# A routed mixture of experts with a gated recurrence on one core: seventeen early pairs instead of eighteen, a setup without transfers between partitions, and two statistics moved

## The reference

```python
combined = xn @ W_in + b_in                      # 256 + 8 columns
embed, state_in = combined[..., :256], combined[..., 256:]
gate = sigmoid(combined @ W_g + b_g)             # 8 columns
state[t] = gate[t] * state[t-1] + (1 - gate[t]) * state_in[t]
s = concat(embed, states) @ W_out + b_out
# mixture of experts: 32 experts, 4 per token, from the best 4 of 8 groups
w, idx = gate_top_k(softmax(xn @ wg.T))          # weights sum to one
# an expert takes at most 1280 rows, in the order of the tokens
y = sum over experts of w * (silu(xe @ w1) * (xe @ w3)) @ w2
z = (silu(xn @ sw1) * (xn @ sw3)) @ sw2          # shared expert
out = x + s * silu(y + z)
```

## Time and profile before

| | |
|---|---|
| three runs | 1102.82, 1106.45, 1108.12 us (median 1106.45) |
| the profiled execution | 1105.46 us, its span 1103.5 us |
| PE busy | 1003.9 us (91%) |
| DVE, ACT, POOL busy | 775.6 (70%), 550.2 (50%), 721.3 us (65%) |
| mean granted TensorE clock | 0.959 of full speed |
| DMA | 197.5 MB, 179 GB/s over the span |

### The profile page before, as it was taken

The page is one execution under the profiler, slowest core; times in us unless marked ns, Lnnn a source line. Parts: engine busy times, 40 slices in busy tenths (PEclk is TensorE's granted clock), DMA queues, the critical chain, the costliest instruction groups (busy, mean ns, idle before and its releaser), DMA issues.

```text
span 1103.5 us, 29611 instructions
## 1 busy us (share of the span) xinstructions
PE 1003.9 (91%) x8031; PEld 957.7 (87%) x8031; DVE 775.6 (70%) x2472; ACT 550.2 (50%) x1039; POOL 721.3 (65%) x564
## 2 busy tenths in 40 slices
PE   7899999999860899899999999999999999999784
PEld 5888888988760899899999999999999999999741
DVE  5888888887760577677777766776777777777574
ACT  4776778777530344344444434444444444445343
POOL 2077777777777766765787876666666667666340
PEclk8899999999995799999999999999999999999987
DMA  9634444444343898787888988898788988877969
GB/s 261 208 127 143 142 143 143 141 149 143 133 145 126 267 234 171 145 196 156 179 168 185 212 157 169 181 202 175 156 186 201 204 203 188 181 145 153 248 152 345
DMA packets 177521, 197.50 MB, mean 179 GB/s; under 512 B 20449, under 2 KB 169234, under 8 KB 177426
## 3 DMA queue, kind: packets, MB, share of 16 engines
q1 hardware_dynamic: 123344, 124.92, 38.0%
q0 software_dynamic: 53440, 71.50, 34.3%
q10 hardware_dynamic: 642, 0.02, 0.0%
HBM read 96.88 MB, written 103.13 MB: 181 GB/s over the span
## 4 chain that ended last, share of the span: by engine, by line
PE 62%; POOL 16%; issue 7%; DVE 6%; DMA 3%; ACT 2%; SPq 1%; DVEq 0%; POOLq 0%; ACTq 0%
POOL slot_rows L854 16%; PE h L989 12%; PE h L991 12%; PE h L990 12%; PE yb L1007 6%; PE yb L1009 6%; PE yb L1008 6%; PE xt L973 6%; DMA raw<-L_ffn_w 1%; DVE s_all L1976 1%; DMA y_sum<-y_more,y_idx 1%; ACT acth L1319 1%; DVE raw L1601 0%; PE h L1198 0%; PE h L1202 0%
## 5 line engine op out<-in xcount | busy, mean ns | idle before, releaser
L989 PE MATMUL h<-xh,w_hl 128*128 (+1 forms) x1392 | 411.8, 296 | 7.2 <-DVE xl L1578 5.6
L991 PE MATMUL h<-xl,w_hl 128*128 (+1 forms) x1392 | 394.7, 284 | 0.0
L990 PE MATMUL h<-xh,w_hl 128*128 (+1 forms) x1392 | 393.6, 283 | 0.0
L1319 ACT ACTIVATE acth<-act 128x512 fp32r<-128x512 f32 x174 | 109.9, 632 | 334.1 <-PE yb L1009 294.2
L989 PEld LDWEIGHTS h<-xh,w_hl 128*128 128x128 f32 x1392 | 265.2, 191 | 9.3 <-issue 8.8
L990 PEld LDWEIGHTS h<-xh,w_hl 128*128 128x128 f32 x1392 | 265.4, 191 | 0.0
L991 PEld LDWEIGHTS h<-xl,w_hl 128*128 128x128 f32 x1392 | 265.1, 190 | 0.0
L1588 DVE TENSOR_TENSOR actl<-act,acth 128x512 fp32r<-128x512 f32 x174 | 120.6, 693 | 178.4 <-ACT acth L1319 178.1
L1007 PE MATMUL yb<-w_hl,acth 128*128 128x256 f32 x696 | 200.3, 288 | 13.3 <-DVE y_more L1848 7.4
L834 POOL DMA_INDIRECT y_sum<-x_all,y_idx x98 | 156.1, 1593 | 73.5 <-DVE x_all L1848 48.6
L1009 PE MATMUL yb<-w_hl,actl 128*128 128x256 f32 x696 | 198.4, 285 | 0.0
(11 more groups left out here) (238 smaller groups left out, 1591.4 us busy)
## 6 DMA issues: line engine op xcount, KB each, us to landing
rows<-slot_rows SPq DMA_DIRECT2D x121, 289.0 KB, 3.9
raw<-L_ffn_w SPq DMA_DIRECT2D x105, 256.0 KB, 4.1
slot_rows<-rows SPq DMA_DIRECT2D x32, 289.0 KB
x_all<-L_attn_x SPq DMA_DIRECT2D x16, 512.0 KB, 6.3
x_all<-L_attn_x SPq DMA_DIRECT2D x32, 256.0 KB
out<-s_all SPq DMA_DIRECT2D x32, 256.0 KB, 4.0
y_sum<-yw SPq DMA_DIRECT2D x31, 256.0 KB
x_all<-slot_rows SPq DMA_DIRECT2D x21, 289.0 KB, 4.2
```

The costliest lines, as they stand in the source:

```text
L989: mm(out, high, xh[:, k, cols], start=(k == 0), stop=False)
L990: mm(out, low, xh[:, k, cols], start=False, stop=False)
L991: ins = mm(out, high, xl[:, k, cols], start=False, stop=(k == KD - 1))
L1319: av(acth[:, :], act[:, :], ACT.Copy).then_inc(acth_ready, 2)
```

## The change

- Expert 0 has two early pairs instead of three; its third pair is done in the late stage, ahead of its last. The y buffers of early and late pairs move accordingly, and so do the waits for them.
- The zero stores of the early experts are issued one expert at a time between the loads, in place of four together and then two.
- POOL waits for a group's four indices at once, in place of one tile at a time.
- The low part of the bias goes into row 64 of `wo`, which DVE can write itself, and the rows 0 to 15 are made in one DVE instruction from two loaded copies of the eight rows: high part times +1 or -1, plus the copy times 0 or 1, by columns that POOL's iota gives. Both transfers and their wait go.
- The statistics of groups 2 and 3 stand in the setup on DVE, and the first half of group 1's normalisation behind the second pair's `xhigh` on ACT.
- `SOON` is 16 in place of 20.

```diff
-SOON = 20
+SOON = 16
-EARLY_PAIRS = 3 * FIRST
+EARLY_COUNTS = (2, 3, 3, 3, 3, 3)
+EARLY_LIST = [(e, j) for e in range(FIRST) for j in range(EARLY_COUNTS[e])]
+EARLY_PAIRS = len(EARLY_LIST)
...
-        LATE_FIFTH, LATE_LAST = (SET_A + 3, SET_A + 4), (SET_A + 1, SET_A + 2)
+        LATE_THIRD = SET_A + 1
+        LATE_FOURTH = (SET_A, SET_A, SET_A + 2, SET_A + 3)
+        LATE_LAST = (SET_A + 2, SET_A + 3, SET_A + 4, SET_A + 1)
...
+        def early_splits(e, j):
+            return (2,) if j == 2 else (j,) if j < EARLY_COUNTS[e] - 1 else (1, 2)
+        def early_adds(e):
+            return 32 * (EARLY_COUNTS[e] - (e == 0))
...
-            sp.dma_start(s_wout8, w_out[D:D + SD, :]).then_inc(setup_loaded, 16)
+            for n in range(2):
+                sp.dma_start(s_wout16[n * SD:n * SD + SD, :], w_out[D:D + SD, :]).then_inc(setup_loaded, 16)
...
-            for e in range(PREFILLED, FIRST):
-                store_zeros(e)
-            load_early(5)
+            store_zeros(2)
+            load_early(5, sp.snap(zeros))
             load_raw(2, 1)
-            load_early(6, sp.snap(zeros))
             load_raw(2, 2)
+            load_early(6)
+            store_zeros(3)
+            load_raw(3, 0)
             load_early(7)
...
             for g in range(GROUPS):
                 slot = g % SLOTS
+                hold(dispatch_ready, GT * g + GT)
                 for t in range(GT):
-                    hold(dispatch_ready, GT * g + t + 1)
...
-                    if p == 0:
-                        pe.wait_ge(bias_moved, 32)
...
-            done(av(wo[0:SD, :], s_wout8, ACT.Copy))
+            done(av(high16.bitcast(F32R), s_wout16, ACT.Copy))
...
-            sc.dma_start(wo[97:98, :].bitcast(F32), bias_low).then_inc(bias_moved, 16)
-            sc.dma_start(wo[SD:SD2, :].bitcast(F32), wout8_low).then_inc(bias_moved, 16)
...
             variances(1)
+            statistics(2)
+            done(v.tensor_scalar(is_low, is_low, float(SD), None, ALU.is_ge))
+            ve.wait_ge(setup_dve, 2)
+            done(v.tensor_scalar(is_high, is_low, -2.0, 1.0, ALU.mult, ALU.add))
+            ve.wait_ge(setup_loaded, 48)
+            done(v.tensor_scalar(rest16, s_wout16, is_low, None, ALU.mult))
+            statistics(3)
+            variances(2)
+            ve.wait_ge(setup_dve, 4)
...
-            done(v.tensor_tensor(wout8_low.bitcast(F32R), s_wout8, wo[0:SD, :].bitcast(F32), ALU.subtract))
+            done(v.scalar_tensor_tensor(wo[0:SD2, :], high16, is_high, rest16, ALU.mult, ALU.add))
...
-            done(v.tensor_tensor(bias_low.bitcast(F32R), ls[0][0:1, 0:D], wo[96:97, :].bitcast(F32), ALU.subtract))
+            done(v.tensor_tensor(wo[64:65, :], ls[0][0:1, 0:D], wo[96:97, :].bitcast(F32), ALU.subtract))
...
             recurrence(0, 0, True)
-            statistics(2)
             states_low(0, 0)
-            statistics(3)
-            variances(2)
...
+            def late_free(e):
+                return apart_added[e], 32 * count.flag_behind(e) + late_adds(e)
...
+            last_free = [(added[0][2], 32 * uses), (added[0][3], 32 * uses), (fifth_added, fifth_adds(section_fifths)), late_free(0)]
+            fourth_free = [(first_added, first_adds(E)), late_free(0), late_free(0), late_free(1)]
```

More of the change, by code:

```diff
@@ L242, in build @@
         s_one = carve(1, 1)
-        bias_low = carve(1, D)
-        wout8_low = carve(SD, D)
+        high16, rest16 = carve(SD2, D), carve(SD2, D)
+        is_low = carve(SD2, 1)
+        is_high = carve(SD2, 1)
         s_norm = [carve(P, BATCH_GROUPS * GT) for _ in range(3)]
@@ L878, in _ @@
             add_early(1)
-            add_early(2)
             pool.wait_ge(fifth_added, 32)
-            pool.wait_ge(apart_added[0], 32 * 2)
-            for e in range(1, FIRST):
-                if e == FIRST - 1:
+            pool.wait_ge(apart_added[0], early_adds(0))
+            for q in range(EARLY_COUNTS[0], EARLY_PAIRS):
+                e, j = EARLY_LIST[q]
+                if e == FIRST - 1 and j == 0:
                     pool.wait_ge(counts_ready, 3)
                     count.load_flags()
[L886 to L889, removed]
+                add_early(q)
+                if j == EARLY_COUNTS[e] - 1 and e < FIRST - 1:
+                    pool.wait_ge(apart_added[e], early_adds(e))
             behind_fifth = count.flag_behind(FIRST - 1)
@@ L1184, in _ @@
                     splits_ready(E)
-                step(slot, e, next_fills(E, e), 1 - slot, split=E + e if e > 0 else None)
+                if e == 0:
+                    step(slot, 0, next_fills(E, 0), 1 - slot)
+                    step(slot, 1, next_fills(E, 1), slot)
+                elif e < LATE - 1:
+                    step(slot, e + 1, next_fills(E, e + 1), 1 - slot, split=E + e)
+                else:
+                    step(slot, 0, next_fills(E, 0) + 1, 1 - slot, split=E + e)
                 with pe.If(count.flag_behind(e) > 0):
@@ L1355, in _ @@
             states_high(0, 0)
-            normalise(1, range(2))
             for p in range(A_PAIRS):
@@ L1361, in _ @@
                     xhigh(p + 1, region(1 - i), (h3_ready, p) if p > 0 else None)
+                if p == 0:
+                    normalise(1, range(2))
                 if p > 0:
@@ L1419, in section @@
                 slots(sc, count, body)
[L1421 to L1425, removed]
+            for e, j in EARLY_LIST:
+                if e < FIRST - 1:
+                    pair(early_splits(e, j), (e + 1) % 2, e * 16 + 32, j == 0)
+                else:
+                    pair()
             sc.wait_ge(counts_ready, 3)
@@ L1720, in mark_late @@
             def mark_late():
-                ends = [needed[:, (e * AHEAD + 1) * GROUPS + 1:(e * AHEAD + 2) * GROUPS - 1] for e in range(LATE)]
+                ends = [needed[:, n * GROUPS + 1:(n + 1) * GROUPS - 1] for n in (e * AHEAD + EARLY_COUNTS[e] - 2 for e in range(LATE))]
                 for other in ends[1:]:
@@ L1925, in _ @@
             for q in range(EARLY_PAIRS):
-                e, n = divmod(q, 3)
-                splits = dict(splits=(n,), w_next=(e + 1) % 2, split=e * 3 + 7, after_down=n == 0) if e < FIRST - 1 else {}
+                e, j = EARLY_LIST[q]
+                splits = (dict(splits=early_splits(e, j), w_next=(e + 1) % 2, split=e * 3 + 7, after_down=j == 0)
+                          if e < FIRST - 1 else {})
                 home = ((early_home(0), last_z_stored, 16) if q == 1 else
                         (early_home(1), z_stored, 16 * (A_PAIRS - 1)) if q == 2 else (early_home(q - 1),))
-                pair(*next_early(q), ((q - 1) // 3, *home) if q else None, **splits)
+                pair(*next_early(q), (EARLY_LIST[q - 1][0], *home) if q else None, **splits)
                 if q == 3:
@@ L1969, in _ @@
                         pair(None, 0, before)
-            take_y_before(count.now(), LATE - 1, *late_home(LATE - 1, LATE_LAST, uses))
+            take_y_before(count.now(), LATE - 1, LATE_LAST[LATE - 1], *last_free[LATE - 1])
             ve.wait_ge(x_again, 16 * CHUNKS)
@@ L1983 @@
 SETUP_ACT = 9
-SETUP_DVE = 10
+SETUP_DVE = 13
 DVE_CONSTS = 11
```

111 lines of the change are left out of this document (53 added, 58 removed).

## The result

The changed kernel takes 1095.23 us (median of 11 runs, 1089.34 to 1098.00), the kernel before 1104.37 on the same chip (11 runs, 1099.34 to 1108.12): the ratio is 0.9902, its 95% interval 0.9882 to 0.9922. It is about 1% faster, 9.1 us between the medians, and the forecast was 1095. The profiled execution after took 1093.52 us, its span is 1091.7, its mean granted clock 0.967.

The account below looks back on a forecast made before the run. POOL's scatters held up TensorE's rows at pair 2, with POOL's adds some six pairs behind. From 1105.46 us, 12.9 kept by TensorE and 2.6 lost in the tail gave 1095.2, forecast as 1095, range 1085 to 1102.

Parts of the forecast that it names:

- The 29.8 us go, and what is late next: TensorE's idle at pair 2 vanishes; despite new smaller delays it reaches the sections 31 us earlier, about 35 with head and lesser waits.
- pair 17: The last early pair needs all scatters, so TensorE waits about 6 us for its rows near 400 us.
- The hole: New TensorE idle at (8,3), forecast at some 20 us, in place of the 29.8 at pair 2.
- What stops it: At (8,3) VectorE waits for (6,3)'s add to land; TensorE can gain only the 11.3 us margin plus POOL's gain.
- What POOL gains: POOL's add of (6,3) comes 2.4 us earlier, bounds 6 earlier to 10 later; y of (8,3) thus 13.7 earlier.
- Contention: The 24 scatters between 328 and 358 us now share with loads and VectorE: pitch 1.357 instead of 1.28, costing 1.8 us.
- second rival: All 24 scatters stretch to 1.79 us each, POOL 12.2 later instead of 1.8: total 1105.6 us; chance 0.09.
- Restart: After the wait at (8,3): 2.1 us from one more pair's up products, 2.9 lost to half clock; net 0.8 lost.
- Head: Setup work moved into VectorE's wait before `gate_bias`: net 0.8 us earlier, bounds 4.3 earlier to 3 later.
- Late stage and tail: At the end, last sums 7.3 us later, 4.7 back from fewer transfers behind them: net +2.6, bounds -1 and +6.
- No wait: Rival: nothing stops TensorE at (8,3), it keeps 35 us: 1073 us; chance 0.07.
- Zero stores: Rival: zero stores on SP's queue delay loads, TensorE 14.5 us later: 1123 us; sign, waits over 20 us in 330-400; chance 0.05.

Follow-up runs that it names:

- e1: Changed kernel, with VectorE's wait at a section's fifth pair looking back four experts for fifth-pair adds instead of two: 1077.55 us, ratio 0.973 to the kernel before.
- e2: Changed kernel, with VectorE's fifth-pair wait tightened to the adds of all fifth pairs before its own section: 1118.7 us, ratio 1.0085 to the kernel before.
- e5: Changed kernel, with other y homes for late pairs, so (1,3) doesn't wait for expert 0's adds: 1086.63 us, ratio 0.9866 to the kernel before, 4 runs.
- e6: Changed kernel with `SOON` 20 again instead of 16: 1101.3 us, ratio 0.9962 to the kernel before.
- e7: Changed kernel with both the edits of e1 and e5: 1069.43 us, ratio 0.9692 to the kernel before.
- e3: Kernel before, with only the looser fifth-pair wait of e1: 1106.36 us, ratio 0.9997 to the kernel before.
- e4: Kernel before, with only the change's new setup (head); eighteen early pairs and POOL's single waits kept: 1104.06 us, ratio 0.9976 to the kernel before.
- e8: Changed kernel with the old head (output weights' last rows copied by DMA, statistics of groups 2 and 3 unmoved): 1096.4 us, ratio 0.9933 to the kernel before.

## Why the prediction was right, step by step

**The 29.8 us go, and what is late next.** The wait for pair 2 is gone, as forecast. For PE left to itself 31 us were worked out, and 30.5 are there from (4,3) to (8,2), but not by the terms that were added. The 6 us that I had counted for pair 17, (5,3), did not come: its rows left SP at 404.97, and PE transposed them at 409.04 without a wait. In front of it PE lost more than the 2 that I had counted (below, zero stores). The lead is 35.3 until (5,1); then (5,2) (8.39 from y to y) and (4,3) (9.42) take 4.8 more than before (6.47 and 6.50). At both places PE stands in both kernels, once where it loads the flags of the fifth pairs, once for the rows of (6,1). PE's timeline and windows after:

```profile
409.04 0.60 PE L992 MATMUL xt<-ident,x_all 128*128 128x128 f32 x4
...
414.33 0.39 PE L1008 MATMUL h<-xh,w_hl 128*128 x1 [1.84 <-issue]
...
434.93 0.66 PE L992 MATMUL xt<-ident,rows 128*128 128x128 f32 x4 [2.80 <-DMA rows<-slot_rows]
417.00:419.00 2.00, 2.00 (x11) 2.00 (x11) 0.89 (x2) 0.60 (x1) 1.19 (x1) 0.50 0.99 198
436.00:438.00 2.00, 2.00 (x12) 2.00 (x11) 1.02 (x2) 0.35 (x1) 0.00 (x0) 0.52 0.97 301
```

The same places before:

```profile
449.31 0.38 PE L989 MATMUL h<-xh,w_hl 128*128 x1 [1.54 <-issue]
...
466.90 0.66 PE L973 MATMUL xt<-ident,rows 128*128 128x128 f32 x4 [1.43 <-DMA rows<-slot_rows]
451.00:453.00 2.00, 2.00 (x19) 2.00 (x18) 0.23 (x2) 1.10 (x2) 1.64 (x2) 1.00 0.57 66
468.00:470.00 2.00, 2.00 (x19) 2.00 (x18) 0.99 (x2) 0.33 (x1) 1.07 (x1) 1.00 1.16 218
```

Longer waits are 1.7 of the 4.8 (0.3 and 1.4). Most of the rest is the clock: behind each wait PE runs for some 3 us at 0.50 (1.2 GHz) in this execution, where it stayed at 1.00 (2.4 GHz) before. That is not the change's: in the five other profiles with the same instructions up to there (e1, e2, e5, e6, e7) the two intervals sum to 12.7 to 15.0, here to 17.8, and in e3, which has the early pairs of the kernel before, to 15.4 against 13.0. Those of them that run to (8,2) without a stop have its y at 498.27 to 502.96, 31.1 to 35.8 ahead of before. So one profile can't decide between the 31 and the "about 35" with head and lesser waits, and that 31 and 30.5 agree is in part luck. The hole is 12.2 us and not 20 for two reasons of like size: the lead is 4.5 short of 35 here, and y of (8,3) comes 4.4 earlier than forecast (below).

**What stops it.** Right, in place and cause: y of (8,3), released by a `y_sum` transfer, clock 0.50 (1.2 GHz) behind it. e1 takes the wait away and gets the time, e3 shows that the kernel before does not have it, the table shows y going with the add.

**What POOL gains.** This term was mis-sized: forecast 2.4, measured 6.2 (523.38 against 517.17). The landing was 2.46, not 3.2. Together y of (8,3) is 18.1 earlier, not 13.7. Expert 1's first add is 4.4 earlier, 0.7 of it from expert 0's first and 3.7 from the moved pair (3.78 forecast). Most of the difference need not be the change's: e3 has the scatters, the early adds and the setup of the kernel before word for word, and its (6,3) add ends at 519.74, 3.6 earlier than in the profile of before; in e4 it ends at 519.26. By e3's rows the margin that was put at 11.3 would have been 17.0 (its y of (8,3) is written at 539.97). The base was one execution, and where POOL is in it varies by more than the terms that I added to it.

**Contention.** 1.8 was forecast for the 24 scatters, from a pitch of 1.357 in place of 1.28. Between 328 and 358 it is 1.356 after and 1.285 before, in all seven profiles with seventeen early pairs 1.337 to 1.390 and in the three with eighteen 1.285 to 1.286: right. What of it is VectorE's work and what the loads', no run took apart. The second rival's sign, a pitch over 1.45, does not occur.

**Restart.** 0.8 was forecast; 18.1 fall to 16.8 at (9,0): 1.3 lost, with the clock at 0.50 to about 524.

**Head.** 0.8 and a hold of 0.4 were forecast, 0.4 net. The one pair of profiles says 1.7, but this goes with how far TensorE was in the setup (below): where the setup is fast, the old head has its first scatter at 55.95 and 55.94 and the new one at 55.63 to 55.83, 0.1 to 0.3 earlier with the hold counted in; where it is a little slower, 57.52 and 55.42. The block that was moved ended at 17.74, near 18 as forecast, and DVE then did not wait for `gate_bias` in this profile (0.87 in e2).

**Late stage and tail.** Forecast +7.3 and -4.7. From y of (31,4) to the last add 50.9 us became 58.5: +7.6. e5 takes 3.9 of it back by another home for y of (1,3), whose wait I had put at 1.5. From the last add to the end 38.6 became 35.2: -3.3. The net cost is 4.3 in place of 2.6, and 3.2 more was kept (16.1 in place of 12.9), so the errors cancel in part: 10.3 less was forecast, the two profiled executions lie 11.9 apart and the medians 9.1. That the median is 1095.23 where the sum gave 1095.2 is luck; the mechanism is not.

**Rivals.** *No wait* would have given 1073; e1, where there is none, has 1077.6 and keeps 32.7 at (31,4) where the rival had 35. *Zero stores*: what PE loses in front of (2,0) sums to 10.3 us (11.04, 7.08 and 6.34 from y to y, against 4.71), half of the 20 that I had set as the sign of this rival. The two waits that PE shows are not for rows: 3.69 at 335.21 for the split of expert 1's matrices (forecast as 2), 2.21 at 354.19 behind the flags for the fifths, which DVE makes from 350.24 to 352.65. Most of the other 4.4 is the clock, 0.50 from 335 to 340 and 0.74 from 355 to 360.

**Signs.** Four of those named did not come as said: one wait between 320 and 400 is over 3 us (3.69), pair 17 has none, the hole is 12.2 and not about 20, and the first scatter is at 55.83, in front of 56.5. (6,3)'s add ends at 517.17, not near 521.

**What stays open.** Why POOL's adds stand up to 10 us apart in runs with the same instructions. The first scatter gives 2.2 of it; the rest arises where POOL waits for an expert's adds to land (3.2 to 4.8 at (1,0), 5.5 to 7.5 at (5,0)) and in single long scatters. No run took these apart. Nor does a run have the zero stores or POOL's wait for four indices changed by themselves: what they are worth is not shown.

## What to carry to other kernels

When an engine off the path is far behind and a stop on the path goes, look for the next place where the two meet, and count it from the engine behind: the gain there is the margin of that wait plus what the engine behind gains, and the rest of the removed idle comes back as a new wait. Ask of such a wait whether it waits for what it needs: here for a buffer used four sections ago, by a count taken two sections ago. And a margin read from one execution carries that execution's own luck; take it from several if a term of it is smaller than they differ.

## What the runs showed of the hardware that was not expected

TensorE's clock in the setup is not the same in each execution, and neither is it behind the waits at 414 and 434 (above). Columns as above, first the kernel after, then e2, which has the same instructions there:

```profile
10.00:14.00 4.00, 4.00 (x29) 2.93 (x28) 2.20 (x12) 0.94 (x4) 0.00 (x0) 1.00 1.08 350
14.00:18.00 4.00, 1.45 (x8) 0.58 (x6) 3.85 (x25) 3.06 (x8) 0.00 (x0) 1.00 1.09 353
```

```profile
10.00:14.00 4.00, 4.00 (x14) 3.39 (x12) 2.25 (x12) 0.99 (x4) 0.00 (x0) 0.50 1.06 351
14.00:18.00 4.00, 4.00 (x18) 2.11 (x19) 3.85 (x25) 0.00 (x0) 0.00 (x0) 0.50 1.09 353
```

At 0.50 (1.2 GHz) PE does 14 matmuls in the four microseconds in which it does 29 at 1.00 (2.4 GHz), and the setup ends later. All ten profiles, by the matmuls of that first window, the clock of the second, and the first scatter (in before, e4 and e7 the clock of the first window is 1.00, so their lower counts there are not the clock's):

| kernel | head | matmuls 10 to 14 | clock 14 to 18 | first scatter |
|---|---|---|---|---|
| after, e1, e5 | new | 29 | 0.87 to 1.00 | 55.83, 55.63, 55.80 |
| e7 | new | 23 | 0.68 | 55.97 |
| e4 | new, no hold by group | 18 | 0.74 | 55.42 |
| e2, e6 | new | 14 | 0.50 | 58.04, 58.05 |
| e3, e8 | old | 28, 29 | 0.89, 1.00 | 55.95, 55.94 |
| before | old | 19 | 0.74 | 57.52 |

In these profiles the new head hides a setup that is late by a little, which the old one passes on (57.52, one profile), and not one that is late throughout. What decides the clock there, no run tells. A gain of 2 us in this setup is no larger than the 2.2 by which the first scatter differs between executions of the same instructions there (55.83 and 58.04).
